# A PE loop moved by 60 instructions, and two weight loads moved from GpSimd's queue to SyncE's, in a two-layer cross-attention decoder

## The chip, the cores and the metric

The kernel runs on one core of one Trainium2 chip. The metric is the device time of one execution in microseconds. Below, PE is TensorE (PEld its weight loads), DVE is VectorE, ACT is ScalarE, POOL is GpSimd and SP is SyncE; a small q behind an engine's name is its sequencer, which handles registers, waits, branches and the issue of DMAs.

## The reference

Two layers on 64 independent sequences of 256 rows and 256 columns, each with a context of 77 rows; all in float32.

```python
# layer 0: RMS norm, cross attention over the context, 16 heads of 64
q = rms_norm(x) @ wq ; k = ctx @ wk ; v = ctx @ wv
x = x + softmax(q k^T) v @ wo                       # wo: 1024 x 256
# layer 1: 16 heads of 16
x = x + mha(ln1(x), ln1(x), causal) @ m_proj_w + m_proj_b
x = x + mha(ln2(x), ctx) @ c_proj_w + c_proj_b
x = x + relu(ln3(x) @ f_w1 + f_b1) @ f_w2 + f_b2    # f_w2: 1024 x 256
```

## The kernel before

A setup loads all weights and splits most of them into a high and a low part, so that one exact product is three products of the fast kind (the helper `three`, L997 to L999: high by high, low by high, high by low). Then the sequences are worked on one after another in a software pipeline of three stages: a hardware loop (`Fori`, L409) of 61 turns, in which each turn does some steps for one sequence, some for the one before and some for the one after it. Shortened pieces of the same order stand ahead of the loop and behind it.

The order of the steps of a turn is written out by hand in three tables, one for PE, POOL and SP (`LOOP_ORDER_TEXT`) and one each for ACT and DVE. Every engine has its own program and walks through its table; they meet through semaphores: `full[s]` says that PE has filled PSUM bank s, `free[s]` that its reader is done. The turn of PE begins with the step pv.1.1 (probabilities times values of the causal attention; the products of L1186 and L1193) and ends with f2.1, a product of 1024 rows.

Two products have 1024 rows of weights: wo (steps wo.0 and wo.1, about a third into the turn) and f2 (steps f2.0 and f2.1, its end). Their split weights don't both fit on the chip. They share the tiles `tail_h` and `tail_l`, 1 MB each: the setup stores both pairs in DRAM (`parted`), and each pair is fetched anew in every turn. POOL does that. Its helper `load_parts` (L534 to L537) issues two DMAs. For f2 it does so when both wo products are done (L565 to L572, behind a tiny operation on the tile `passed`, L570). For wo it does so behind the second `xr` operation of the turn (L555), long after f2's products of the turn before have ended.

POOL's other work is small. `inverse_root` (L531) computes the inverse standard deviation for a norm whose variance DVE has just written; L555 adds a bias row to xs and writes xr, and L561 adds one to x. The tile xr is at the same time the output tile y: DVE adds the f2 product to it (L940), SP stores it to `out` (L496), and POOL may write xr again (L555) only when that store has landed (`y_stored`). SP's other DMAs load x twice (tiles xin and x) and the context (cin).

PE's program has in front of the loop the products that fold norms and biases into the weights (L950 to L974), then a wait for `consts_ready`, then the first sequences' steps.

Of the kernel before, what the change touches and what calls it, by code (L numbers as in the profile page):

```python
# [5 lines left out]
ALU = mybir.AluOpType  # L6
# [7 lines left out]
P = 128  # L14
# [218 lines left out]
def decoder(nc, x, ctx, w, out):  # L233
# [27 lines left out]
    with ExitStack() as stack:  # L261
# [27 lines left out]
        small = sb("small", [P, 20])  # L289
        parity, minus_half, msq = small[:, 0:2], small[:, 2:4], small[:, 4:6]  # L290
        veps, rstd = (small[:, a:a + 6].rearrange("p (s t) -> p s t", t=TT) for a in (6, 12))
        passed = sb("passed", [P, TT])
        bias_h, minus_bias = sb("bias_h", [P, MF]), sb("minus_bias", [P, MF])
        qbias = sb("qbias", [P, 2, KT])
        kbias = sb("kbias", [P, 2, KT, 2])
# [155 lines left out]
        @block.sync  # L451
        def _(sp):
            small = [(gain, "gains"), (shift, "shifts"), (bias, "biases"), (bias_h[:], "f1b"), (wk0[:], "wk0"),
                     (wck[:], "ck")]
            for tile, n in small:
                src = w[n]
                if n in ("wk0", "ck"):
                    src = src.rearrange("(k p) n -> p k n", p=P)
                sp.dma_start(tile, src).then_inc(consts_in, 16)
            sp.dma_start(row[:, :, :], w["rows"].unsqueeze(0).to_broadcast([P, 3, C])).then_inc(consts_in, 16)  # L460
            for i, (n, _g, _s) in enumerate(WEIGHTS):
                if i >= 2:

                    sp.wait_ge(w_free[i % 2], i // 2)
                    sp.wait_ge(w_bias, i - 1)
                sp.dma_start(staged(i), w[n].rearrange("(k p) n -> p k n", p=P)).then_inc(w_in[i % 2], 16)
            sp.dma_start(xin[:], x_v[0]).then_inc(x_in, 16)
            sp.dma_start(x1[:], x_v[0]).then_inc(xres_in, 16)
            sp.dma_start(cin[0:S, :], ctx[0]).then_inc(c_in, 16)

            def store_parts(n, value):
                i = [m for m, _, _ in WEIGHTS].index(n)
                sp.wait_ge(w_free[i % 2], i // 2 + 1)
                sp.dma_start(parted[n][0], tail_h[:].bitcast(F32)).then_inc(parts_out, 16)
                sp.dma_start(parted[n][1], tail_l[:].bitcast(F32)).then_inc(parts_out, 16)
                sp.wait_ge(parts_out, value)

            store_parts("wo0", 32)
            store_parts("f2", 64)
            def run(order, c, batch):  # L480
                for step in order:
                    b, u, n = batch[stage_of(step)], c.next(step), step[0]
                    more = not isinstance(b, int) or b + 1 < NB
                    if step == ("turn", 0) and more:
                        sp.wait_ge(x_used, b + 1)
                        sp.dma_start(xin[:], x_at(x_v, b + 1)).then_inc(x_in, 16)
                    elif n == "ctx" and more:
                        sp.wait_ge(c_used, b + 1)
                        sp.dma_start(cin[0:S, :], context_at(b + 1)).then_inc(c_in, 16)
                    elif n == "proj" and step[1] == 1 and ("proj", 1, 1 - step[2]) in c.seen and more:  # L490

                        sp.wait_ge(x1_used, b + 1)
                        sp.dma_start(x1[:], x_at(x_v, b + 1)).then_inc(xres_in, 16)
                    elif n == "f2" and (n, 1 - step[1]) in c.seen:
                        sp.wait_ge(y_ready, b * 2 + 2)
                        sp.dma_start(x_at(out_v, b), y[:]).then_inc(y_stored, 16)  # L496

            def x_at(tensor, b):
                if isinstance(b, int):
                    return tensor[b]  # L500
                return tensor[bass.ds(b, 1)].rearrange("a p t c -> (a p) t c")

            def context_at(b):
                return ctx[b] if isinstance(b, int) else ctx[bass.ds(b, 1)].rearrange("a s c -> (a s) c")

            orders(sp, run)
            sp.wait_ge(y_stored, 16 * NB + 16)


        @block.gpsimd  # L510
        def _(pool):

            nc.gpsimd.memset(ident[:], 0.0).then_inc(consts_made, 1)
            nc.gpsimd.memset(causal[:], 0.0).then_inc(consts_made, 1)
            nc.gpsimd.memset(causalT[:], 0.0).then_inc(consts_made, 1)
            nc.gpsimd.memset(minus_half[:], -0.5).then_inc(consts_made, 1)
            nc.gpsimd.memset(vc[:], 0.0).then_inc(consts_made, 1)
            nc.gpsimd.memset(v1[:], 0.0).then_inc(consts_made, 1)
            nc.gpsimd.memset(k0bd[:], 0.0).then_inc(consts_made, 1)
            pool.wait_ge(consts_made, 7)  # L520
            nc.gpsimd.affine_select(out=ident[:], in_=ident[:], compare_op=ALU.not_equal, fill=1.0, base=0,
                                    pattern=[[-1, P]], channel_multiplier=1).then_inc(consts_made, 1)

            nc.gpsimd.affine_select(out=causal[:], in_=causal[:], compare_op=ALU.is_ge, fill=MASKED, base=0,
                                    pattern=[[-1, P]], channel_multiplier=1).then_inc(consts_made, 1)
            nc.gpsimd.affine_select(out=causalT[:], in_=causalT[:], compare_op=ALU.is_ge, fill=MASKED, base=0,
                                    pattern=[[1, P]], channel_multiplier=-1).then_inc(consts_made, 1)

            def inverse_root(stage, ready, ts):
                pool.wait_ge(stat_ready[stage], ready)  # L530
                nc.gpsimd.tensor_tensor(rstd[:, stage, ts], veps[:, stage, ts], minus_half[:, ts],  # L531
                                        ALU.pow).then_inc(rstd_ready[stage], 1)

            def load_parts(kind):  # L534
                n = "wo0" if kind == "wo" else "f2"
                nc.gpsimd.dma_start(tail_h[:], parted[n][0]).then_inc(tail_in[kind], 16)
                nc.gpsimd.dma_start(tail_l[:], parted[n][1]).then_inc(tail_in[kind], 16)  # L537

            pool.wait_ge(parts_out, 64)
            load_parts("wo")  # L540

            def run(order, c, batch):
                for step in order:
                    b, u, n = batch[stage_of(step)], c.next(step), step[0]
                    if n == "rms":
                        inverse_root(0, b + 1, slice(0, TT))
                    elif n == "stat":
                        k, t = step[1:]
                        inverse_root(*norm_place(k, b, t), slice(t, t + 1))
                    elif n == "norm" and step[1] > 1:  # L550
                        k, t = step[1:]
                        if k == 2 and t == 0:
                            pool.wait_ge(y_stored, b * 16 + 16)
                        pool.wait_ge(stat_ready[1], norm_place(k, b, t)[1])
                        nc.gpsimd.tensor_tensor(xr[:, t, :], xs[:, t, :], row[:, k - 1, :], ALU.add).then_inc(xr_ready, 1)  # L555
                        if step == ("norm", 2, 1) and ("wo", 0) in order:
                            load_parts("wo")
                    elif n == "norm" and step[1] == 1:
                        t = step[2]
                        pool.wait_ge(norm_ready[2], b * 2 + t + 1)  # L560
                        nc.gpsimd.tensor_tensor(x1[:, t, :], x1[:, t, :], row[:, 0, :], ALU.add).then_inc(x1_ready, 1)  # L561
                    if n in ("wo", "f2") and (n, 1 - step[1]) in c.seen:
                        done = {s: v for st in order if st[0] == n for s, v, _ in c.of[st]["bank"]}
                        for s, v in done.items():
                            pool.wait_ge(full[s], v)  # L565

                        later = [st[0] for st in (order if n == "wo" else ()) if st[0] == "f2"]
                        later += [st[0] for st in c.after if st[0] in ("wo", "f2")]

                        nc.gpsimd.tensor_tensor(passed[:], minus_half[:], minus_half[:], ALU.mult)  # L570
                        if later and not (later[0] == "wo" and ("norm", 2, 1) in c.after):
                            load_parts(later[0])  # L572

            orders(pool, run)


# [373 lines left out]
        def _(pe):  # L950
# [3 lines left out]
            for i, (n, g, s) in enumerate(WEIGHTS):  # L954
# [17 lines left out]
                    ins.then_inc(bias_products, 1)  # L972

                pe.drain().then_inc(w_bias, 1)  # L974
            pe.wait_ge(consts_ready, 1)
            for bank_full in full:
                pe.sem_inc(bank_full, FIRST)
# [286 lines left out]
```

## Time and profile before

| | |
|---|---|
| time before, median of 3 runs | 5510.0 us (5502.45 to 5510.83) |
| profiled execution, its own time | 5519.77 us |
| its span in the profile | 5517.8 us |
| busy share PE, PEld, DVE, ACT, POOL | 90%, 75%, 67%, 75%, 13% |
| mean granted clock of PE | 0.963 |
| DMA | 348.70 MB, 63 GB/s on average |

The span reaches from the first to the last instruction of the profiled execution. Busy time is that of an engine's operations; registers, branches, semaphores and the issue of DMAs are not in it. The granted clock is the share of TensorE's full clock, 2.4 GHz, that the chip let it have; 0.5 is 1.2 GHz.

### The profile page before, as it was taken

The numbers are of one execution on the slowest core, as the hardware profiler recorded it, in microseconds if no ns is written. First come the engines' busy times: TensorE is split into PE (matmuls) and PEld (weight loads), VectorE is DVE, ScalarE is ACT, GpSimd is POOL, SyncE is SP. The second block draws the span as 40 slices with busy tenths as digits, with TensorE's granted clock in tenths as the row PEclk, the third lists the DMA queues.
The fourth block names the chain that finished last, engine by engine and source line by source line (L and its number), as shares of the span: only waits on it lengthen the run. The fifth ranks groups of instructions, "written<-read, shape, count | busy, mean of one in ns | idle before, by whom it ended". The sixth has DMA issues, their size and how long they took to land. (4 is left out here: it accounts for less than half of the span.)

```text
span 5517.8 us, 148465 instructions
## 1 busy us (share of the span) xinstructions
PE 4964.5 (90%) x47704; PEld 4162.7 (75%) x47704; DVE 3680.1 (67%) x9511; ACT 4142.7 (75%) x17025; POOL 704.6 (13%) x1230
## 2 busy tenths in 40 slices
PE   5899999999999999999999999999899999999996
PEld 4677777777777777777777777777777777777775
DVE  4666666666666667667666666676676666666774
ACT  2787787787777777777877877777778778777785
POOL 0111111111111111111111111111111111111111
PEclk8999999999999999999999999999999999999998
DMA  3112121121121121121211211211211112112111
GB/s 119 46 66 73 43 73 60 56 74 60 57 73 60 54 76 55 59 75 43 72 61 56 73 60 55 76 60 54 75 46 69 69 47 73 60 57 73 60 54 52
DMA packets 102243, 348.70 MB, mean 63 GB/s; under 512 B 8752, under 2 KB 66928, under 8 KB 68080
## 3 DMA queue, kind: packets, MB, share of 16 engines
q0 software_dynamic: 36864, 268.45, 13.3%
q1 hardware_dynamic: 64496, 68.39, 3.8%
q8 instruction: 565, 9.26, 0.7%
q14 instruction: 318, 2.61, 0.2%
HBM read 315.84 MB, written 20.97 MB: 61 GB/s over the span
## 5 line engine op out<-in xcount | busy, mean ns | idle before, releaser
L600 ACT ACTIVATE ps<-ps,negmax 128x77 f32<-128x77 f32 (+2 forms) x6144 | 2053.7, 371 | 231.8 <-DVE negmax L822 219.7
L600 ACT ACTIVATION_READ_ACCUMULATOR ps<-ps,negmax 128x1 f32 x6144 | 1464.1, 249 | 1.5
L822 DVE TENSOR_REDUCE negmax<-ps 128x4 f32<-128x308 f32 (+2 forms) x1792 | 945.9, 564 | 165.6 <-PE ps L1086 93.1
L997 PE MATMUL ps<-tail_h,coTh 128*128 128x256 f32 x2048 | 594.3, 290 | 4.2 <-DVE coTl L930 2.0
L998 PE MATMUL ps<-tail_l,coTh 128*128 128x256 f32 x2048 | 573.9, 280 | 0.0
L999 PE MATMUL ps<-tail_h,coTl 128*128 128x256 f32 x2048 | 572.8, 280 | 0.0
L531 POOL TENSOR_TENSOR small<-small 128x1 f32<-128x1 f32 (+1 forms) x448 | 265.4, 592 | 2283.5 <-DVE small L789 2059.2
L580 ACT CAST zTh<-ps 128x256 fp32r<-128x256 f32 x512 | 203.0, 397 | 470.1 <-PE ps L1193 356.1
L675 ACT ACTIVATE probs<-ps 128x512 f32<-128x512 f32 x768 | 405.7, 605 | 140.2 <-DVE ps L814 140.1
L997 PEld LDWEIGHTS ps<-tail_h,coTh 128*128 128x128 f32 x2048 | 385.9, 188 | 43.6 <-issue 26.3
L807 DVE TENSOR_TENSOR zTl<-ps,zTh 128x256 fp32r<-128x256 f32 x512 | 213.4, 417 | 298.0 <-ACT zTh L580 298.0
L1086 PE MATMUL ps<-k0bd,q0T 128*128 128x154 f32 x2048 | 392.8, 338 | 2.6 <-ACT probs L675 2.5
L998 PEld LDWEIGHTS ps<-tail_l,coTh 128*128 128x128 f32 x2048 | 386.7, 189 | 0.0
L999 PEld LDWEIGHTS ps<-tail_h,coTl 128*128 128x128 f32 x2048 | 386.5, 189 | 0.0
L814 DVE TENSOR_TENSOR ps<-ps,causal 128x256 f32<-128x256 f32 (+1 forms) x768 | 370.2, 513 | 8.3 <-PE ps L1110 1.9
L814 DVE TENSOR_TENSOR ps<-ps,causalT 128x256 f32<-128x256 f32 (+1 forms) x768 | 341.4, 513 | 50.5 <-PE ps L1158 50.5
L1086 PEld LDWEIGHTS ps<-k0bd,q0T 128*128 128x128 f32 x2048 | 338.0, 222 | 26.3 <-issue 23.0
L580 ACT COPY probs<-ps 77x512 f32<-77x512 f32 x512 | 287.4, 623 | 62.3 <-PE ps L1125 62.3
L671 ACT ACTIVATE probs<-ps 77x512 f32<-77x512 f32 x512 | 254.4, 601 | 79.0 <-PE ps L1140 79.0
L997 PE MATMUL ps<-zTh,hi_f 128*128 128x256 f32 x1024 | 299.3, 292 | 1.7 <-issue 1.0
L570 POOL TENSOR_TENSOR passed<-small 128x2 f32<-128x2 f32 x128 | 24.6, 192 | 2159.0 <-PE ps L999 2159.0
L997 PE MATMUL ps<-xTh,hi_wq 128*128 128x256 f32 x1024 | 287.6, 281 | 2.5 <-DVE xTl L807 1.5
(199 smaller groups left out, 13046.3 us busy)
## 6 DMA issues: line engine op xcount, KB each, us to landing
tail_h<-parted_wo POOLq DMA_DIRECT2D x64, 1024.0 KB, 5.2
tail_l<-parted_wo POOLq DMA_DIRECT2D x64, 1024.0 KB, 7.1
tail_h<-parted_f POOLq DMA_DIRECT2D x64, 1024.0 KB, 5.4
tail_l<-parted_f POOLq DMA_DIRECT2D x64, 1024.0 KB, 7.2
xin<-x_dram SPq DMA_DIRECT2D x64, 256.0 KB, 3.2
x<-x_dram SPq DMA_DIRECT2D x64, 256.0 KB, 2.7
out<-xr SPq DMA_DIRECT2D x64, 256.0 KB, 2.2
cin<-ctx_dram SPq DMA_DIRECT2D x64, 77.0 KB
```

Source lines behind the costliest of these rows:

```text
L531: nc.gpsimd.tensor_tensor(rstd[:, stage, ts], veps[:, stage, ts], minus_half[:, ts], ALU.pow).then_inc(rstd_ready[stage], 1)
L580: return nc.scalar.copy(o, i)
L600: ins = nc.scalar.activation(scores, scores, ACT.Exp, bias=negmax[w][:, t, h:h + 1], accum_out=sums[w][:, t, h:h + 1])
L671: nc.scalar.activation(probs_slot(step, r)[0:S], bank(s)[0:S, :], ACT.Exp).then_inc(free[s], 1)
L675: nc.scalar.activation(probs_slot(step, r), bank(s), ACT.Exp).then_inc(free[s], 1)
L807: nc.vector.tensor_tensor(lo, src, hi, ALU.subtract).then_inc(free[s], 1)
L814: nc.vector.tensor_tensor(scores, scores, tile[:].unsqueeze(1).to_broadcast([P, heads, P]), ALU.add).then_inc(added, 1)
L822: nc.vector.tensor_reduce(dst, bank(s)[:, 0:heads * width].rearrange("p (h k) -> p h k", h=heads), AX_X, ALU.max, negate=True).then_inc(ma ...
L997: pe.matmul(o, lh, rh, start=first, stop=False)
L998: pe.matmul(o, lh, rl, start=False, stop=False)
L999: return pe.matmul(o, ll, rh, start=False, stop=last)
L1086: ins = pe.matmul(bank(s)[:, j * 2 * S:(j + 1) * 2 * S], q0T[:, m, t * P:(t + 1) * P], k0bd[:, m, :, :], start=True, stop=True)
```

## The change

PE gets 120 waits at the end of the setup's products, ahead of the wait for `consts_ready`. They wait for a value that has been reached since the setup's first loads, and the compiler of the program packs two waits into one instruction: 60 instructions.

The loads of `tail_h` and `tail_l` go from POOL's program to SP's. SP issues the first pair right behind the stores of the setup; the pair for f2 when the banks of both wo products are full, as before; and the pair for wo when DVE has written both halves of y, directly ahead of the store of y. POOL's operation on `passed` and its waits for PE's banks go.

```diff
@@ SP, behind the setup's stores
+            def load_parts(kind):
+                n = "wo0" if kind == "wo" else "f2"
+                for half, tile in enumerate((tail_h, tail_l)):
+                    sp.dma_start(tile[:].bitcast(F32), parted[n][half]).then_inc(tail_in[kind], 16)
+
+            load_parts("wo")
@@ SP, run
+                    elif n == "wo" and (n, 1 - step[1]) in c.seen:
+
+                        for t in range(TT):
+                            s, v, _ = c.of[("wo", t)]["bank"][0]
+                            sp.wait_ge(full[s], v)
+                        later = [st[0] for st in order if st[0] == "f2"] + [st[0] for st in c.after if st[0] in ("wo", "f2")]
+                        load_parts(later[0])
                     elif n == "f2" and (n, 1 - step[1]) in c.seen:
                         sp.wait_ge(y_ready, b * 2 + 2)
+                        later = [st[0] for st in c.after if st[0] in ("wo", "f2")]
+                        if later:
+                            load_parts(later[0])
                         sp.dma_start(x_at(out_v, b), y[:]).then_inc(y_stored, 16)
@@ POOL, ahead of the loop
-            def load_parts(kind):
-                n = "wo0" if kind == "wo" else "f2"
-                nc.gpsimd.dma_start(tail_h[:], parted[n][0]).then_inc(tail_in[kind], 16)
-                nc.gpsimd.dma_start(tail_l[:], parted[n][1]).then_inc(tail_in[kind], 16)
-
-            pool.wait_ge(parts_out, 64)
-            load_parts("wo")
@@ POOL, run
-                        if step == ("norm", 2, 1) and ("wo", 0) in order:
-                            load_parts("wo")
-                    if n in ("wo", "f2") and (n, 1 - step[1]) in c.seen:
-                        done = {s: v for st in order if st[0] == n for s, v, _ in c.of[st]["bank"]}
-                        for s, v in done.items():
-                            pool.wait_ge(full[s], v)
-
-                        later = [st[0] for st in (order if n == "wo" else ()) if st[0] == "f2"]
-                        later += [st[0] for st in c.after if st[0] in ("wo", "f2")]
-
-                        nc.gpsimd.tensor_tensor(passed[:], minus_half[:], minus_half[:], ALU.mult)
-                        if later and not (later[0] == "wo" and ("norm", 2, 1) in c.after):
-                            load_parts(later[0])
@@ PE, end of the setup
                 pe.drain().then_inc(w_bias, 1)
+
+
+            for _ in range(120):
+                pe.wait_ge(consts_in, 16 * 7)
             pe.wait_ge(consts_ready, 1)
```

SP's program from the second xin load of a turn to the turn's end, before: xin and cin are the next loads, out is the store of y.

```order
L486 DMA xin<-x_dram 128x2x256
L489 ISA [waits c_used]
L489 DMA cin<-ctx_dram 77x256
L495 ISA
L496 ISA [waits y_ready]
L496 DMA out<-xr 128x2x256
L409 REGISTER_ALU
L409 COMPARE_BRANCH
```

The same stretch in the change; full2 and full5 are the banks of wo.0 and wo.1.

```order
L493 DMA xin<-x_dram 128x2x256
L505 ISA
L505 ISA [waits full2]
L483 DMA tail_h<-parted_f 128x2048 [waits full5]
L483 DMA tail_l<-parted_f 128x2048
L496 ISA [waits c_used]
L496 DMA cin<-ctx_dram 77x256
L509 ISA
L483 DMA tail_h<-parted_wo 128x2048 [waits y_ready]
L483 DMA tail_l<-parted_wo 128x2048
L513 ISA
L513 DMA out<-xr 128x2x256
```

The load for f2 stands ahead of the load of cin, and the load for wo between the wait for y and the store of y.

POOL's program in the turn, before, from the second xr operation (step norm.2.1) to the second inverse root of the norm behind wo (stat.1.1).

```order
L555 TENSOR_TENSOR xr<-xs,row 128x256 [waits stat_ready1]
L536 DMA tail_h<-parted_wo 128x2048
L537 DMA tail_l<-parted_wo 128x2048
L530 ISA
L531 TENSOR_TENSOR small<-small 128x1 [waits stat_ready2]
L561 TENSOR_TENSOR x<-x,row 128x256 [waits norm_ready2]
L565 ISA
L565 ISA [waits full2]
L570 TENSOR_TENSOR passed<-small 128x2 [waits full5]
L536 DMA tail_h<-parted_f 128x2048
L537 DMA tail_l<-parted_f 128x2048
L531 TENSOR_TENSOR small<-small 128x1 [waits stat_ready2]
```

The same stretch in the change.

```order
L564 TENSOR_TENSOR xr<-xs,row 128x256 [waits stat_ready1]
L547 ISA
L548 TENSOR_TENSOR small<-small 128x1 [waits stat_ready2]
L568 TENSOR_TENSOR x<-x,row 128x256 [waits norm_ready2]
L547 REGISTER_ALU
L548 TENSOR_TENSOR small<-small 128x1 [waits stat_ready2]
```

The four DMAs, the waits for PE's banks and L570 are gone. PE's own steps keep their order; PE's loop begins 60 instructions further on.

## Rows read from the trace of the kernel before

**Rows 1.** The page: busy us by engine, share of the span, instructions.

```profile
PE 4964.5 (90%) x47704; PEld 4162.7 (75%) x47704; DVE 3680.1 (67%) x9511; ACT 4142.7 (75%) x17025; POOL 704.6 (13%) x1230
```

**Rows 2.** Waits: engine, line, releaser, us in total, times, longest us.

```profile
ACT zTh L580 <- PE ps L1193: 356.1, 66, 6.2
...
PE ps L1186 <- issue: 141.2, 61, 4.2
PE ps L1193 <- issue: 78.2, 60, 1.9
```

**Rows 3.** Line 409, the loop's branch: ns min/median/max, first and last start.

```profile
L409 PEldq COMPARE_BRANCH  x61: 83/3667/3887, 255.3 to 5293.2; - x61
```

**Rows 4.** PE in time order around a turn's edge: start us, us, operation, [idle before].

```profile
2693.27 1.12 PE L1186 MATMUL ps<-probs,v 128*32 128x256 f32 x16 [2.33 <-issue]
...
2695.71 0.85 PE L1193 MATMUL ps<-probs,v 128*32 128x128 f32 x9 [0.90 <-issue]
```

**Rows 5.** Queue q8 in 2689.7:2692.5 and in 848.26:930.08: packets, MB, share.

```profile
q8 instruction: 1, 0.02, 3.0%
...
q8 instruction: 9, 0.15, 0.8%
```

**Rows 6.** PE's register instructions at the loop's head, from 2692 on.

```profile
L409 PEldq FUSED_REGOPS  x1: 50/50/50, 2692.6 to 2692.6; - x1
...
L993 PEldq FUSED_REGOPS  x4: 37/37/37, 2692.7 to 2693.0; - x4
L993 PEldq ALU_OP  x2: 32/34/36, 2693.1 to 2693.2; - x2
```

**Rows 7.** PE in time order at the edge of a full-speed turn.

```profile
849.15 0.40 PE L1193 MATMUL ps<-probs,v 128*32 128x128 f32 x7
850.68 0.51 PE L1193 MATMUL ps<-probs,v 128*32 128x128 f32 x9 [1.13 <-issue]
```

**Rows 8.** Windows: length, busy us (count) by engine, granted clock, DMA share, GB/s.

```profile
2696.60:2700.60 4.00, 4.00 (x17) 4.00 (x18) 1.65 (x4) 2.53 (x16) 0.00 (x0) 0.50 0.01 4
...
2693.27:2777.20 83.93, 77.54 (x744) 65.06 (x745) 56.92 (x147) 64.77 (x266) 10.91 (x19) 0.96 0.18 62
848.26:930.08 81.82, 74.71 (x744) 62.65 (x745) 56.65 (x147) 64.76 (x266) 10.96 (x19) 1.00 0.18 64
```

**Rows 9.** The turn from 2693.27 in time order: SP, POOL, DVE, PE.

```profile
2691.57 0.40 SPq L496 DMA_DIRECT2D out<-xr  x1
...
2702.32 0.73 POOL L555 TENSOR_TENSOR xr<-xs,row 128x256 f32<-128x256 f32 x1
2704.86 0.54 POOL L531 TENSOR_TENSOR small<-small 128x1 f32<-128x1 f32 x1 [1.81 <-DVE small L789]
...
2728.93 0.41 DVE L798 TENSOR_SCALAR z<-x,mv,small 128x256 f32<-128x256 f32 x1 [0.97 <-POOL small L531]
...
2731.59 0.44 PE L1005 MATMUL ps<-ident,z 128*128 128x128 f32 x2
```

**Rows 10.** The end of the setup: POOL, DVE, PE; the row of L1228 has 16 waits.

```profile
74.30 0.75 POOL L531 TENSOR_TENSOR small<-small 128x2 f32<-128x2 f32 x1
...
70.49 0.16 DVE L786 SCALAR_TENSOR_TENSOR small<-small,mv 128x2 f32<-128x2 f32 x1
75.08 0.61 DVE L796 TENSOR_SCALAR xin<-xin,small 128x256 f32<-128x256 f32 x2 [4.43 <-POOL small L531]
...
75.84 1.09 PE L1005 MATMUL ps<-ident,xin 128*128 128x128 f32 x4 [15.29 <-DVE xin L796]
...
L1228 PEldq EVENT_SEMAPHORE  x16: 51/51/2810, 172.4 to 176.8; - x16
```

**Rows 11.** DMA issues of the whole span: KB each, median us to landing.

```profile
tail_l<-parted_wo POOLq DMA_DIRECT2D x64, 1024.0 KB, 7.1
...
out<-xr SPq DMA_DIRECT2D x64, 256.0 KB, 2.2
...
probs<-wo_dram SPq DMA_DIRECT2D x1, 1024.0 KB, 5.5
```

More of the change, by code:

```diff
@@ L291, in decoder @@
         veps, rstd = (small[:, a:a + 6].rearrange("p (s t) -> p s t", t=TT) for a in (6, 12))
-        passed = sb("passed", [P, TT])
         bias_h, minus_bias = sb("bias_h", [P, MF]), sb("minus_bias", [P, MF])
```

## Prediction

> **What bounds the kernel now.** I read the page first, then the waits of TensorE, then one turn of the loop in time order, and only then what the moved loads touch. The page makes PE the engine to watch: busy for 90% of the span [rows 1]. The loop runs 61 turns; from its first backward branch to its last, 60 turns, it takes 5293.2 - 255.3 = 5037.9 us, or 83.97 us a turn [rows 3]. Among PE's waits the reader is to see that the two largest have no releaser: "issue", 141.2 us in front of the products at L1186 and 78.2 us in front of those at L1193, each about once a turn [rows 2]. PE waits there for no engine and no data.
>
> The branch says where. PE's COMPARE_BRANCH takes 3667 ns in the median turn and 83 ns the one time that it falls through [rows 3]. In a usual turn the first matmul behind it starts at 2693.27, after 2.33 us of idleness; then 16 products of L1186 and 7 of L1193 run, and PE stops again for lack of instructions [rows 4, 7]. In the first stop the trace has one packet of the instruction queue q8 [rows 5], and one again in the stretch of the second (2692.5 to 2695.5). So the first stop is the fetch of the block that the branch jumps to, and the second that of the block behind it, which PE reaches too soon. Between the loop's head and the second stop there are 1 + 4 + 2 register and wait instructions [rows 6], 23 weight loads and 23 matmuls: 53 instructions.
>
> Third, the clock. Behind the branch the granted clock falls to half, 0.50 over four microseconds in which PE is busy throughout [rows 8]. A few turns escape it: the one from 848.26 to 930.08 ran at clock 1.00 and took 81.82 us, the one from 2693.27 to 2777.20 at 0.96 and 83.93 us, with the same 744 matmuls [rows 7, 8]. So the slow clock costs about 2.1 us a turn.
>
> **The change, part by part.** *60 instructions ahead of the loop.* The 120 waits are for a value long reached and are packed two to an instruction: 60. They push every later PE instruction 60 places on. The boundary that lay 53 places behind the head now finds the head 7 places beyond it, in the first places of a block. The branch still fetches one block (2.33 us idle, unchanged), but the next boundary is a whole block away. A turn takes 9 packets of q8 for 1488 loads and matmuls [rows 5, 8], so a block holds at least 165 instructions, some 80 matmuls; PE is through these more than 10 us after the head, and a fetch with its wait took at most the 3.89 us of the longest branch [rows 3]. That stop goes. Its worth: in the full-speed turn PE was idle for 1.13 us [rows 7], and since the matmul in front is counted to its modelled end, some 0.22 us after its successor could have started (7 in 0.40 us), I take 1.35 us. The ends are 1.13 and 850.68 - 849.15 = 1.53 us. What follows hangs on PE there: ScalarE idles up to their end, 356.1 us in all and 6.2 at the longest [rows 2], so all of it moves up.
>
> *The clock.* The stop that stays is 2.33 us of idleness, the one that goes about half as long. I take the fall as caused by the idleness around the edge, and expect the first to be enough for one half-speed stretch in nearly every turn, but a shorter one than the 0.04 x 2 x 83.9 = 6.7 us of the usual turn. Now a part of the slow stretch lies over the second stop and costs nothing; afterwards all of it lies over work. A stretch of half today's length, 3.4 us, over work costs 1.7 us instead of 2.1. I take 0.3 us as the gain, between a loss of 1.3 (6.7 us at half speed, all over work, 3.35 us instead of 2.1) and a gain of 2.1 (no fall).
>
> *The 60 instructions' own time.* Sixteen such waits stand 0.11 us apart [rows 10], so 60 take 6.5 us. PE's last product of the setup ends near 60.5, and its first transpose starts at 75.84 after 15.29 us of waiting for DVE [rows 10]; that covers them. Without the cover they would cost 6.5 us, once.
>
> *POOL loses the loads.* Before the loop POOL waits until the split weights are stored, issues two DMAs and only at 74.30 computes the first inverse root, whose input DVE had ended at 70.65; DVE waits 4.43 us for it [rows 10]. Freed, POOL can answer at 70.7: 3.6 us earlier, and PE's first transpose with it. Bounds 0 and 3.6; I take 3.5, once. In a turn, L570 and the two issues stand in front of the root of stat.1.1, for which DVE waits 0.97 us [rows 9]. DVE gets that back, but the transpose that needs the result starts at 2731.59 behind other products and waits for nothing: worth zero. The cover there is 2.2 us (2731.59 less the 2729.34 at which DVE is done).
>
> *SP gets them.* For the second-layer weights (f2) SP waits for the banks of both wo products, stands in front of the load of cin only, which waits for a later step of the turn anyway, and delays nothing. The wo weights now start when y is ready, at the turn's edge, instead of behind POOL's second xr operation, which follows the root at 2704.86 [rows 9]: they can only come earlier to a product that waits for no weights today (none of PE's waits names them). Behind them in SP's queue stands the store of y, issued at 2691.57 today and landed 2.2 us on. POOL waits for it before it overwrites xr at 2702.32 [rows 9]. Two DMAs of 1 MB have landed 7.1 us after the second's issue when POOL issues them; one 1 MB load by SP took 5.5 [rows 11]. With 7.1 the store lands near 2691.6 + 0.8 + 7.1 + 2.2 = 2701.7, and POOL, moved up by 1.65, wants it at 2700.7. It may be 1.0 us late; but POOL's next result that DVE needs is the root at 2704.86 (2703.2 then), and 0.73 + 1.0 fit in front of it. Cost zero; how much more would cost is in the rivals.
> Here the page "DMA: Bandwidth & Descriptors" of the Trainium skill (Queues, rings and completion order) speaks against the change: SP owns one ring on each of the same 16 engines, consumed in order, so the store queues behind 2 MB, whereas (SWDGE vs HWDGE vs iDMA) GpSimd's and SP's DMAs sit in different internal queues that the engine serves in turn. No row of before can show it, since SP never queued a store behind such a load.
>
> *Sum.* 60 turns x (1.35 + 0.3) = 99 us, and 3.5 of the start: 102.5 us. Against the profiled execution's 5519.8 us that is 5417.3; it stood 0.18% over the median of 5510.0, so the median should come to 5407.
>
> **The Trainium skill on the fetch.** The page "Runtime: NRT & Kernel Launch" (Instruction fetch mechanics) says that blocks are fetched ahead in sequence, that a taken branch to a block not held waits for it, and that crossing a boundary is mostly hidden. It also gives PE room for 2048 instructions: by that a turn would stay resident, nothing would be fetched and the change would bring nothing. The trace disagrees on that point, with 9 packets a turn and a 3.67 us branch.
>
> **The rivals.** (1) *As summed*, 0.74: 5407, own range 5375 to 5440. (2) *The clock no longer falls*, since idleness at the edge shrinks from some 3.5 to 2.33 us, 0.06: 60 x (1.35 + 2.1) + 3.5 = 210 us, 5300. Against it: 2.33 us stay, and the half-speed stretch lies right behind them. (3) *The slow stretch keeps its length* and lies over work, 0.07: 60 x (1.35 - 1.3) + 3.5 = 7 us, about 5503; with half of that loss 5464. (4) *The second stop stays*, the boundary not being where I count it or blocks being fetched otherwise, 0.04: 5506. (5) *The head falls in front of a boundary instead of behind it*, were my count short by 8 or more, 0.04: PE then stops for a second whole fetch, up to 3.6 us in place of 1.35, 60 x 2.2 = +135 us less 3.5, 5640. (6) *The store behind the 2 MB*, 0.05, slower: with 5.5 us for each MB the store lands at 2691.6 + 0.8 + 11 + 2.2 = 2705.6, 4.9 us after POOL wants it. POOL has 2703.2 - 0.73 - 2700.7 = 1.8 us of slack, so 3.1 us a turn reach DVE and PE: 60 x (3.1 - 1.65) = +87 us, about 5590. It decides once the store lands more than 1.8 + 1.65 = 3.4 us after POOL's wish, that is after 2704.1.
>
> **How the numbers follow.** The likeliest case gives 5407. No change can be told within 0.2%, 11 us, on either side of 5510. Faster: cases 1 and 2 and most of 3, 0.85. Same: the rest of 3 and case 4, 0.06. Slower: cases 5 and 6, 0.09. The range reaches down to 5365, for a stop worth 1.53 us and a clock gain of 0.85, and up to 5495, into case 3; case 2 below and 4, 5 and 6 above stay out, 0.19.
>
> **What the profile of after would show.** The wait for issue at L1193 gone from PE's waits and the one at L1186 still near 2.3 us a turn; the branch still near 3.6 us; turns of about 82.3 us, with a shorter half-speed stretch in each; the first root of POOL near 70.7; no wait of POOL for the store of y over 1.8 us. I would be wrong if a stop for instructions appears at another line, if PEclk over the loop doesn't rise, or if POOL's L564 (L555 of before) waits for out<-xr by more than that.

## The result, and the profile after

The change made the kernel faster by far more than I had forecast: 5253.6 us (median of 4 runs, 5249.33 to 5259.63) against 5510.4 us (4 runs, 5502.45 to 5518.80) on the same chip, a ratio of 0.9535 with a 95% interval of 0.9518 to 0.9552. The forecast was 5407, with a range from 5365 to 5495. The profiled execution took 5259.63 us.

The page of after: its span, the busy time of the engines, the granted clock over 40 slices of the span, the queue q8 that fetches PE's instructions, and two DMAs with KB and us to landing.

```profile
span 5257.0 us, 148335 instructions
...
PE 4855.7 (92%) x47704; PEld 4066.1 (77%) x47704; DVE 3686.0 (70%) x9511; ACT 4162.1 (79%) x17025; POOL 539.6 (10%) x846
...
PEclk8999999999999999999999999999999999999997
...
q8 instruction: 25, 0.41, 0.0%
...
tail_l<-parted_wo SPq DMA_DIRECT2D x64, 1024.0 KB, 7.4
out<-xr SPq DMA_DIRECT2D x64, 256.0 KB, 7.5
```

The page of before had 565 packets of q8, and 9 of them fell into one turn [rows 5]. After has 25 in the whole execution. None lies behind the loop's first turn: this is the view of the DMA queues in the window from 249.5 to 5030 us, with packets, MB and share.

```profile
q1 hardware_dynamic: 88894, 304.37, 17.5%
q14 instruction: 301, 2.47, 0.2%
```

The branch of the loop, with least, median and longest ns and first and last start, to be read beside [rows 3]:

```profile
L408 PEldq COMPARE_BRANCH  x61: 76/208/241, 250.8 to 5024.0; - x61
```

It takes 0.21 us instead of 3.67, and 60 turns take 5024.0 - 250.8 = 4773.2 us, 79.55 each instead of 83.97. That is 265 us, and the two profiled executions differ by 5519.8 - 5259.6 = 260 us: the gain is in the turns. The start adds 4.5 us to it (first branch at 250.8 instead of 255.3), and the stretch behind the last branch takes 8.4 us away (5257.0 - 5024.0 = 233.0 us against 5517.8 - 5293.2 = 224.6).

Waits of after, each with us in total, times and longest: the stops for instructions, and three waits that have grown; behind them the first of these as it was in before.

```profile
PE ps L1005 <- DVE z L794: 81.1, 130, 4.5
...
PE ps L1186 <- ACT probs L671: 21.8, 63, 0.6
...
PE ps L1186 <- issue: 4.3, 1, 4.3
...
POOL xr L564 <- DMA out<-xr: 176.0, 63, 3.9
...
PE ps L1005 <- DVE z L798: 32.9, 68, 4.4
```

Both stops of [rows 2] are gone; the single 4.3 us lies at 172.36, at the head of the loop's first turn. In exchange PE now waits 81.1 us in all for z, where the same wait had 32.9 before; its wait for ScalarE's probs at L1186 has grown to 21.8 us, 0.34 a turn; and POOL waits 176.0 us for the store of y, 2.8 us a turn, where it had waited once for 3.2 us.

One edge of the loop in time order (start us, us, operation, [idle before]): PE, SP, POOL and DVE, and then the end of the setup with POOL, DVE and PE.

```profile
2639.44 1.07 PE L1186 MATMUL ps<-probs,v 128*32 128x256 f32 x16 [0.34 <-ACT probs L671]
2640.32 0.63 PE L1193 MATMUL ps<-probs,v 128*32 128x128 f32 x16
...
2650.19 0.44 PE L1005 MATMUL ps<-ident,z 128*128 128x128 f32 x2 [0.73 <-DVE z L794]
...
2639.59 0.33 SPq L483 DMA_DIRECT2D tail_h<-parted_wo  x1
2639.96 0.43 SPq L483 DMA_DIRECT2D tail_l<-parted_wo  x1
2640.57 0.40 SPq L513 DMA_DIRECT2D out<-xr  x1
...
2644.85 0.54 POOL L548 TENSOR_TENSOR small<-small 128x1 f32<-128x1 f32 x1 [2.31 <-DVE small L785]
2648.07 0.72 POOL L564 TENSOR_TENSOR xr<-xs,row 128x256 f32<-128x256 f32 x1 [2.68 <-DMA out<-xr]
2648.75 0.54 POOL L548 TENSOR_TENSOR small<-small 128x1 f32<-128x1 f32 x1
...
2649.32 0.81 DVE L794 TENSOR_SCALAR z<-xs,mv,small 128x256 f32<-128x256 f32 x1 [0.31 <-POOL small L548]
...
71.57 0.71 POOL L548 TENSOR_TENSOR small<-small 128x2 f32<-128x2 f32 x1 [67.18 <-DVE small L782]
...
71.33 0.16 DVE L782 SCALAR_TENSOR_TENSOR small<-small,mv 128x2 f32<-128x2 f32 x1
...
73.07 1.08 PE L1005 MATMUL ps<-ident,xin 128*128 128x128 f32 x4 [10.91 <-DVE xin L792]
```

Compare the first row with [rows 4]: the first matmul behind the branch stood 2.33 us idle and now 0.34, and it waits there for ScalarE, no longer for instructions. The 16 products of L1193 run in one piece. The rows of SP show the store of y issued behind 2 MB of weights; POOL is held 2.68 us by it, the root behind it is late, DVE's z waits 0.31 and PE's transpose 0.73.

The loop as a window, with columns as in [rows 8]:

```profile
260.00:4900.00 4640.00, 4373.04 (x43395) 3663.85 (x43394) 3321.64 (x8573) 3793.78 (x15540) 490.28 (x761) 1.00 0.18 64
```

The granted clock over the loop is 1.00. The half-speed stretch at the turn's edge [rows 8] is gone. In 9 of the 60 turns the clock still falls, for 3.4 us and later in the turn; e3 below bears on that.

### The profile page after: what moved, and what is told of

It is laid out like the page before. It is cut to its first block and busy times, and to the rows that moved or that the text cites. A ratio compares the mean times of both kernels' runs of the same rounds, so it can differ in the third digit from the quotient of the medians.

```text
span 5257.0 us, 148335 instructions
## 1 busy us (share of the span) xinstructions
PE 4855.7 (92%) x47704; PEld 4066.1 (77%) x47704; DVE 3686.0 (70%) x9511; ACT 4162.1 (79%) x17025; POOL 539.6 (10%) x846
## 5 line engine op out<-in xcount | busy, mean ns | idle before, releaser
L576 ACT CAST zTh<-ps 128x256 fp32r<-128x256 f32 x512 | 203.4, 397 | 226.6 <-PE ps L1193 122.4
L1086 PE MATMUL ps<-k0bd,q0T 128*128 128x154 f32 x2048 | 330.4, 299 | 2.5 <-ACT probs L671 2.5
L1086 PEld LDWEIGHTS ps<-k0bd,q0T 128*128 128x128 f32 x2048 | 284.1, 191 | 15.6 <-issue 12.7
L998 PE MATMUL ps<-xTl,hi_wq 128*128 128x256 f32 x1024 | 291.1, 284 | 0.0
L999 PE MATMUL ps<-xTh,lo_wq 128*128 128x256 f32 x1024 | 291.0, 284 | 0.0
```

What stands on the lines that cost most here:

```text
L576: return nc.scalar.copy(o, i)
L998: pe.matmul(o, lh, rl, start=False, stop=False)
L999: return pe.matmul(o, ll, rh, start=False, stop=last)
L1086: ins = pe.matmul(bank(s)[:, j * 2 * S:(j + 1) * 2 * S], q0T[:, m, t * P:(t + 1) * P], k0bd[:, m, :, :], start=True, stop=True)
```

## The experiments

The theory after the result: PE keeps as many blocks of instructions as it needs to hold the whole turn, if the turn lies over 7 of them, and must fetch them all anew in every turn if it lies over 8. With the head 60 places further on, the turn fits. (A block is what one packet of q8 brings.) A turn has 1623 PE instructions (counted in the program: 1488 loads and matmuls and 135 others). In before the boundary is 53 places behind the head; with blocks of 256 the head is at place 203 of its block and the turn ends at 203 + 1623 = 1826, in the 8th block. With 60 more the head is at place 7 and the end at 1630, in the 7th. The size of 256 can be read off the trace: when the last seven packets of q8 in a turn of before begin, PE has started 131, 393, 660, 921, 1102, 1409 and 1606 instructions since the branch (medians, its sequencer's included), on average 246 apart. e5 to e8, e11 and e12 test it more sharply. The rivals: it is the place of the head near the start of a block that counts; or the moved loads bring part of the gain.

Ratios are to the kernel before on the same chip: 5522.3 us beside e1 to e4 (7 runs), and 5522.3 beside e9 to e12 (9 runs). e5 to e8, e11 and e12 were run once and have no ratio; before took 5521.7 beside e5 to e8.

**e1, the waits alone.** Before, with the waits at the same place of PE's setup and POOL's loads as they were:

```diff
                 pe.drain().then_inc(w_bias, 1)
+            for _ in range(120):
+                pe.wait_ge(consts_in, 16 * 7)
```

> The kernel before with the 60 waits alone; POOL still issues the loads. Theory R (residency: a turn's 1623 PE instructions stay in PE's instruction store when the turn spans 7 blocks of 256 and not when it spans 8, so nothing is fetched in the loop): no q8 packets between the first turns and the loop's end, the branch near 0.2 us, no idleness for issue at L1186 and L1193, clock near 1.00, a turn of 81.82 - 1.99 - 1.35 = 78.5 us, in all 5510 - 60 x 5.47 = about 5182 us, 70 us faster than the full change, since the store of y isn't behind the weights. Rival Q (a good part of the gain comes from the loads' move): this kernel stays clearly slower than the full change, above 5300 us.

Measured: 5210.4 us, ratio 0.9435 (0.9419 to 0.9450). Its branch:

```profile
L409 PEldq COMPARE_BRANCH  x61: 76/208/241, 256.2 to 4977.7; - x61
```

Its store of y, with KB and us to landing:

```profile
out<-xr SPq DMA_DIRECT2D x64, 256.0 KB, 2.2
```

A turn takes (4977.7 - 256.2) / 60 = 78.69 us, and the store lands as fast as in before. The 60 instructions alone bring 5.6% and the whole change 4.65%: all of the gain is theirs, and the moved loads take something back. I had expected a turn of 78.5 us and 5182 us in all; the turn is 0.2 us longer, and before took 12 us more beside it than beside the change.

**e2, the moved loads alone.** After, without the waits:

```diff
-            for _ in range(120):
-                pe.wait_ge(consts_in, 16 * 7)
```

> The full change without the 60 waits: the loads on SP's queue, the loop where it was. Theory R: both stops and the half-speed stretch stay, the store of y lands some 7.5 us after its issue but PE comes later too, so POOL hardly waits and 3.5 us are gained at the start: 5500 to 5512 us. Rival Q: clearly faster than before, under 5450 us.

Measured: 5691.1 us, ratio 1.0306 (1.0289 to 1.0324). I had expected no difference, so this missed, and by a lot. The waits, and an edge in time order:

```profile
PE ps L1190 <- issue: 226.6, 60, 4.3
PE ps L1183 <- issue: 135.4, 61, 4.2
```

```profile
2856.85 1.30 PE L1183 MATMUL ps<-probs,v 128*32 128x256 f32 x16 [2.30 <-issue]
2857.90 0.67 PE L1190 MATMUL ps<-probs,v 128*32 128x128 f32 x7
2861.76 0.85 PE L1190 MATMUL ps<-probs,v 128*32 128x128 f32 x9 [3.19 <-issue]
```

The first stop (L1183 here, L1186 of before) is as it was. The second, at the same 53rd instruction, has grown from 78.2 to 226.6 us, that is by 2.5 us a turn. The DMA queues in the window 2857:2859, then q8 in 2859:2859.7, and last q8 of before in 2693.3:2693.6, say why:

```profile
q1 hardware_dynamic: 100, 0.82, 99.9%
...
q8 instruction: 1, 0.02, 8.9%
...
q8 instruction: 1, 0.02, 21.0%
```

The 2 MB keep the 16 DMA engines busy by 99.9%, and the packet of the second block starts only in the stretch from 2859.0 to 2859.7, 2.1 us or more behind the first matmul at 2856.85; in before it starts between 2693.3 and 2693.6, at most 0.3 us behind the first matmul at 2693.27 [rows 4]. So a data load at the edge delays the code that PE needs there; e9, which moves that load alone, confirms it. With the turn resident there is no code to delay, and the same load costs 1% instead of 3%.

**e3, the store of y ahead of the loads.** After, with two lines exchanged:

```diff
                         sp.wait_ge(y_ready, b * 2 + 2)
+                        sp.dma_start(x_at(out_v, b), y[:]).then_inc(y_stored, 16)
                         later = [st[0] for st in c.after if st[0] in ("wo", "f2")]
                         if later:
                             load_parts(later[0])
-                        sp.dma_start(x_at(out_v, b), y[:]).then_inc(y_stored, 16)
```

> The full change with SP issuing the store of y ahead of the two wo loads. Theory S (the store queued behind 2 MB makes POOL's xr late, by 2.68 us in a turn, and that reaches PE as 0.82 us in front of the second transpose of z): the store lands in about 2.2 us, the wait of PE for z goes, a turn takes 78.5 us in place of 79.4, in all 5253.6 - 60 x 0.85 = about 5200 us. Rival (that wait of PE comes from DVE's own chain once PE is faster): 5245 to 5260 us, unchanged.

Measured: 5221.8 us, ratio 0.9454 (0.9438 to 0.9470).

Its branch, its store and its wait for z, from three views:

```profile
L408 PEldq COMPARE_BRANCH  x61: 76/208/241, 254.1 to 4994.1; - x61
```

```profile
out<-xr SPq DMA_DIRECT2D x64, 256.0 KB, 2.3
```

```profile
PE ps L1005 <- DVE z L794: 26.7, 68, 2.3
```

The store lands in 2.3 us, POOL's wait for it is no longer among its waits, and PE's wait for z falls from 81.1 to 26.7 us. A turn is 79.00 us against 79.55 of after. So the order of store and loads costs 0.55 us a turn, 33 us in all, and the stretch behind the last branch is back at 5218.5 - 4994.1 = 224.4 us, 8.6 less than in after. Together that is 42 us, and the ratios differ by 0.8%, 45 us. (The start of e3 is 3.3 us longer, first branch at 254.1 against 250.8, and before took 5522 us beside it, 5510 beside after.) I had expected about 5200 us, with 0.85 us a turn for the order, so that missed.

A part of the 0.55 us is the clock. In the turn of after whose first matmul starts at 2240.17, PE's transpose starts at 2251.09 after 0.90 us of waiting for z, and from 2252.6 to 2256.0 the granted clock is 0.51. Nine of after's 60 turns hold such a stretch and take 80.6 us from branch to branch, the others 79.4; e3 has no such turn. That is some 12 of the 33 us. The wait for z is 0.6 to 1.1 us in every turn of after, and in six of the nine the stretch starts only some 10 us behind it, so what makes the clock fall in just these is not shown.

The kernel stays behind e1 by another 0.3 us a turn.

**e4, 213 instructions.** Before, with `range(426)`, 213 instructions. The head comes to place 203 + 213 - 256 = 160, in the middle of a block, and the end to 1783, within 7 x 256 = 1792.

> The kernel before with 213 waiting instructions in place of 60 ahead of PE's loop, so that the head stands 160 places into a block of 256 (203 + 213 - 256) and the turn still ends inside the 7th block (160 + 1623 = 1783 of 1792). Theory R: no fetches in the loop, a time like e1's plus at most 8 us for waits that the setup no longer covers (213 x 0.107 = 22.8 us against 15.3): about 5190 us. Rival H (what matters is that the head stands near the start of a block, as the recorded prediction had it): a boundary 96 places behind the head, the second stop is back, above 5400 us.

Measured: 5219.7 us, ratio 0.9453 (0.9437 to 0.9469), and 26 packets of q8. Its branch:

```profile
L409 PEldq COMPARE_BRANCH  x61: 76/208/233, 264.6 to 4989.2; - x61
```

That is 78.74 us a turn, as in e1; the 9 us over e1 lie ahead of the loop, where 213 waits are no longer covered (first branch at 264.6 against 256.2). I had expected about 5190. The head need not be near the start of a block: that rival falls.

**e5 to e8, the edges of the step.** The same edit with 52, 53, 222 and 223 instructions, run once each. By the count the turn ends at place 1878 (head at 255, 8 blocks), 1623 (head at 0, 7 blocks), 1792 (exactly 7 blocks) and 1793 (one instruction in the 8th).

> The kernel before with 52 waiting instructions in place of 60. By the 53 instructions counted between the head and the second stop, the head is then the last instruction of a block, and the turn spans 8 blocks (1 + 1622). Theory R: still fetched every turn, some 9 packets of q8 a turn, and the second stop is now a whole fetch right behind the head, up to 3.6 us in place of 1.35: 5500 to 5650 us. Rival H2 (it is enough to be near a boundary, or my count is off by a few): 5210 us, like 60.

> One waiting instruction more than e5_align_52: the head is the first instruction of a block, the turn spans 7 blocks. Theory R: no fetches in the loop, 5205 to 5215 us, some 300 to 400 us faster than with 52. Any other theory has no step between 52 and 53.

> 222 waiting instructions: the head 169 places into its block, the turn's last instruction the last of the 7th block (169 + 1623 = 1792 = 7 x 256). Theory R: no fetches in the loop, about 5222 us (as with 213). If PE also needs room ahead of the branch, it is fetched again: above 5400.

> 223 waiting instructions: the turn's last instruction falls into an 8th block. Theory R: 9 packets of q8 a turn again, the branch near 3.6 us, a shorter second stop than before since the next boundary is 86 places behind the head: 5440 to 5540 us. Rival H (position of the head alone): no step between 222 and 223.

Measured: 5609.7, 5206.0, 5217.1 and 5215.9 us. The waits of e5, its queue q8 and its branch:

```profile
PE ps L1188 <- issue: 344.8, 61, 6.1
```

```profile
q8 instruction: 565, 9.26, 0.7%
```

```profile
L409 PEldq COMPARE_BRANCH  x61: 83/3582/3982, 260.3 to 5381.7; - x61
```

The branch of e6, and the queue q8 of e8:

```profile
L409 PEldq COMPARE_BRANCH  x61: 76/208/242, 254.9 to 4976.7; - x61
```

```profile
q8 instruction: 26, 0.43, 0.0%
```

One instruction more, 52 to 53, takes 404 us away. That places the boundary exactly where the count has it, and it shows what a head just in front of a boundary costs: one stop of 344.8 / 61 = 5.65 us, both blocks fetched in full. At the other edge my expectation for e8 missed: with one instruction (the branch itself) in the 8th block the turn is still resident. Eight blocks do fit. Each of the four is a single run, but runs of one kernel here lie within 0.3% (16 us), and branch and q8 show the same two cases.

**e11 and e12, more in the 8th block.** 233 and 243 instructions, that is 11 and 21 in the 8th block, run once each.

> 233 waiting instructions: the turn's last 11 instructions lie in an 8th block (with 223 it was one, and the turn stayed resident; with 0 it is 34 and is fetched). Theory R2 (8 blocks fit; what breaks them is the fetch of the 9th, started as soon as PE has entered the 8th and not yet branched back): with 11 instructions, some 0.6 us of products, the branch may still come first; if so 5217 us and no q8 packets in the loop, else 5450 to 5550.

> 243 waiting instructions: 21 instructions in the 8th block, some 1.2 us of products before the branch. Theory R2: near the point where the fetch of the 9th block starts ahead of the branch (with 34 it starts 0.9 us ahead of it). With 21 I expect it to start about when the branch is taken, and the loop to be fetched again: 5450 to 5600 us, 9 packets of q8 a turn. If it is resident still, 5218 us, and the threshold lies between 21 and 34.

Measured: 5410.3 and 5424.7 us, both a little under the 5450 that I had expected at least if the turn is fetched. The waits of e11, its queue q8 and its branch:

```profile
PE ps L1188 <- issue: 139.2, 61, 4.2
```

```profile
q8 instruction: 566, 9.27, 0.8%
```

```profile
L409 PEldq COMPARE_BRANCH  x61: 83/3633/3937, 265.9 to 5181.9; - x61
```

The waits of e12, its branch, and a window of its loop with the columns of [rows 8]:

```profile
PE ps L1188 <- issue: 143.6, 61, 4.2
PE ps L1195 <- issue: 57.0, 50, 1.7
```

```profile
L409 PEldq COMPARE_BRANCH  x61: 83/3727/3931, 269.9 to 5194.0; - x61
```

```profile
260.00:4900.00 4640.00, 4233.23 (x42103) 3541.34 (x42099) 3206.47 (x8316) 3663.40 (x15052) 620.05 (x1076) 1.00 0.18 64
```

Somewhere between 1 and 11 instructions in the 8th block the turn stops being resident. What fits both sides is this: PE holds 8 blocks and fetches one ahead; once it is far enough into the 8th, it fetches the 9th, the code behind the loop, and that takes the place of the first. In e11 this fetch begins 0.74 us before the branch; e8, at its branch at once, never begins it. The ninth packet does begin near the count's eighth block: when PE has started 1606 instructions of the turn in before (that block begins behind 1589), 1607 in e11 (1612) and 1566 in e5 (1537), all medians. That it takes the place of the first block, and so on through all of them, is argued from these runs, not shown by itself.

e11 is also the kernel that my prediction described: first stop kept, second gone, one short half-speed stretch of 3.4 us in every turn, 5410 us against the 5407 forecast (before took 5522 beside e11, and 5510 beside the change).

**e9 and e10, the loads by SP at their old time.** The wo pair is issued by SP behind its load of x in the step proj.1.1, instead of at the turn's edge; e9 without the 60 waits, e10 with them. The cut shows the new issue; the one at the edge goes.

```diff
                     elif n == "proj" and step[1] == 1 and ("proj", 1, 1 - step[2]) in c.seen:
                         if more:
                             sp.wait_ge(x1_used, b + 1)
                             sp.dma_start(x1[:], x_at(x_v, b + 1)).then_inc(xres_in, 16)
+                        if ("wo", 0) in order:
+                            load_parts("wo")
```

> e2_queue_only with one thing changed: SP issues the wo loads behind its load of x in the next turn (step proj.1.1), near the place where POOL issued them, instead of at the turn's edge. Still no waits, so PE fetches its code in every turn. Theory C (2 MB at the turn's edge hold back PE's second block, whose fetch starts 7.1 us behind the branch in place of 4.7 and lengthens the second stop from 1.3 to 3.8 us; that made e2 slower than before): the second stop is back at 1.3 us and the time at 5500 to 5520 us. Rival D (SP's queue or the hardware's descriptors are slower for PE wherever they stand): 5600 us or more, as e2.

> e9_late_queue with the 60 waits, or the full change with the wo loads issued at proj.1.1 of the next turn. Theory R with S: nothing is fetched and the store of y has nothing in front of it, so e1's turn of 78.7 us, and the earlier first root on top: 5205 to 5212 us. Rival: loads by SP's queue cost PE something wherever they stand, 79.0 us a turn as in e3_store_first: about 5222 us.

Measured: e9 5541.3 us, ratio 1.0036 (1.0023 to 1.0049); e10 5221.4 us, ratio 0.9457 (0.9441 to 0.9472), 79.00 us a turn. The waits of e9, and the branches of e9 and e10:

```profile
PE ps L1186 <- issue: 143.0, 61, 4.2
PE ps L1193 <- issue: 73.3, 60, 1.8
```

```profile
L408 PEldq COMPARE_BRANCH  x61: 83/3727/3891, 252.0 to 5306.0; - x61
...
L408 PEldq COMPARE_BRANCH  x61: 76/208/241, 252.7 to 4992.5; - x61
```

With the 2 MB away from the edge the second stop is 1.2 us a turn again, as in before. So of the 3.1% of e2 all but 0.4% was the load at the edge. The rest stays: wherever SP issues the loads, a turn is some 0.3 us longer than with POOL (84.23 against 83.97 without the waits, 79.00 against 78.69 with them). I had expected e9 at 5500 to 5520 and e10 at 5205 to 5212, and both missed by about this. The 0.3 us are not in PE's waits but in its products: in the window 260:4900, at a granted clock of 1.00 in both, e10 is busy for 4395.4 us with 43643 products and e1 for 4386.6 us with 43863. Why they take longer is open. The edit also takes POOL's operation L570 away and puts the f2 loads ahead of cin, and no run separates these.

The four corners, as ratios to before:

| | loads by POOL | by SP, at the edge | by SP, at the old time |
|---|---|---|---|
| head at place 203 | 1 | 1.0306 | 1.0036 |
| 60 instructions on | 0.9435 | 0.9535 | 0.9457 |

## Why the prediction was wrong

**The step that failed** is the sentence in "60 instructions ahead of the loop": "The branch still fetches one block (2.33 us idle, unchanged)". The prediction's section on the Trainium skill had the rule that would have mended it, from that skill's page "Runtime: NRT & Kernel Launch" (Instruction fetch mechanics): room for 2048 instructions on PE. I wrote "The trace disagrees on that point, with 9 packets a turn and a 3.67 us branch". The trace did not disagree. I had tested the rule for one layout only, without asking how many blocks the turn lies over there: 8, with the fetch ahead of a 9th, by which nothing stayed. The number was in reach, as I knew that 53 instructions lay between head and boundary, and moving the head changes just that count. After 60 instructions the branch takes 0.21 us (after), and with 53 too (e6); with 52 it takes 3.58 (e5). On the room the trace now agrees with the page: 8 blocks of 256. It does not with the same section's sentence on a taken branch, which speaks of a window of two blocks: here a branch back over six block boundaries takes 0.21 us.

**The clock** followed. I kept one half-speed stretch because I kept the first stop, and took 0.3 us for it. Without any stop the stretch goes in nearly every turn, worth the 2.1 us that I had put on rival 2. Of rival 2 the price was right and the cause was not: it was to come from a shorter idleness with the first stop still there. e12 comes near that price from the other side: it has both stops, the clock stays at full speed in 48 of 60 turns, and its turn is (5194.0 - 269.9) / 60 = 82.07 us against before's 83.97. Of these 1.9 us some 0.35 are its shorter second stop (57.0 us in all against 78.2).

**The second stop's price**, 1.35 us, was about right. In e11, which removes it and keeps the first, the turn is (5181.9 - 265.9) / 60 = 81.93 us, 2.04 below before, where the sum said 1.35 + 0.3 = 1.65. How the extra 0.4 divides between stop and clock isn't settled.

**The 60 instructions' own time** was hidden as said: PE's first transpose comes at 73.07 and still waits 10.91 us for DVE.

**POOL loses the loads.** POOL answers at 71.57 instead of 74.30, 2.7 us earlier, and PE starts 2.8 us earlier where I took 3.5. POOL itself is freed as said; DVE's input came 0.84 us later than before (71.33 against 70.49 [rows 10]).

**SP gets them.** I put the store 1.0 us behind POOL's wish and its cost at zero. In the turn shown it lands 8.5 us behind the issue of the first load (2640.57 + 7.5 - 2639.59), where I had summed 10.1. But POOL wants it 5.8 us behind that issue (2648.07 - 2.68 - 2639.59), where I had 9.1: the first stop and the slow clock that went too had moved POOL's wish up. So POOL waits 2.68 us. The slack of 1.8 us does not cover that, and e3 puts the price at 0.55 us a turn and 8.6 us behind the loop. That is the mechanism of rival 6, at 0.55 instead of 3.1 us a turn. The page "DMA: Bandwidth & Descriptors" of the Trainium skill (Queues, rings and completion order), which the prediction set against the change and then priced at zero, agrees with it: the store waits in SP's ring behind the 2 MB, 7.5 us against 2.3 in e3. A further cost I had not listed at all: the load at the edge delays PE's code (e2). What it would have cost with the first stop left, as I forecast, no run shows: e2's first stop is no longer than before, it is the second that grows, and that one was to go. I had excluded only that the loads come too late for their products, not what else uses the DMA engines then.

**The sum as it came out**, per turn: first stop 2.33 - 0.34 = 2.0; second stop 1.3; clock 2.1; against it 0.55 for the store (0.2 of it the clock) and 0.3 for SP's loads. That is 4.55, and 4.42 were measured (83.97 - 79.55); the 0.13 between them is not placed.

The best version measured is e1, the 60 instructions with POOL's loads kept: 5210 us where before has 5522.

## What to carry to other kernels

If the profile shows a hardware loop whose branch takes microseconds and an instruction queue with packets in every turn, count the blocks that the turn's program lies over, from where it starts in its block; a few dozen cheap instructions ahead of the loop may make it resident, and that takes away every stop and what the clock loses behind them. Try such a shift alone and at two or three sizes, since here one instruction decided over 404 us. And when a load is moved to another time or queue, ask what else needs the DMA engines and that queue just then: the store behind it, and the code of an engine that is being fetched.

## What the runs showed of the hardware

- PE kept a turn of 1623 instructions as long as at most one of them lay in the 8th block of 256, and fetched 9 packets a turn when 11, 21 or more did. A branch back took 0.21 us in the first case and 3.6 us in the second.
- A load of 2 MB held the DMA engines at 99.9% and with it a code fetch: the second stop grew from 1.3 to 3.8 us (e2).
- The clock does not fall after every stop. Before has two stops and falls to half; e11 has one of 2.3 us and falls for 3.4 us; e12 has two (2.3 and 1.1 us) and stays at full speed in 48 of 60 turns. After waits 0.6 to 1.1 us for z in every turn and falls in 9 of 60. What tells them apart is open.
